# Flamingo-style block (gated cross-attention, MLP, two FFNs) on Trainium2: value split and row moments of the first stage moved to other engines and a later place

## The reference

```python
def layer0_attention(x, y):                # x is normalised per row first: (x - mean) / sqrt(var + 1e-5)
    q = (x @ Wq + bq)                      # 16 heads of 16
    k = (y @ Wk + bk)                      # 77 context rows
    v = (y @ Wv + bv)
    attn = softmax(q @ k.T / 4)            # per head
    out = attn @ v
    return relu(out @ W1 + b1) @ W2 + b2
# then: layer 0 FFN on fp4-quantised operands; layer 1 attention (own Wq, Wk, Wv, Wo, no biases);
# layer 1 FFN: 8 experts, top 2 per row
```

## Time and profile before

| | |
|---|---|
| Runs | 739.12, 739.69, 741.12 us |
| Profiled execution | 739.43 us, span 737.7 us |
| TensorE busy (PE) | 590.7 us, 80% |
| VectorE busy (DVE) | 542.5 us, 74% |
| ScalarE busy (ACT) | 348.6 us, 47% |
| GpSimd busy (POOL) | 250.2 us, 34% |

### The profile page before, as it was taken

The page is one execution under the profiler, slowest core; times in us unless marked ns, Lnnn a source line. Parts: engine busy times, 40 slices in busy tenths (PEclk is TensorE's granted clock), DMA queues, the critical chain, the costliest instruction groups (busy, mean ns, idle before and its releaser), DMA issues. The chain is left out here.

```text
span 737.7 us, 15590 instructions
## 1 busy us (share of the span) xinstructions
PE 590.7 (80%) x5555; PEld 527.1 (71%) x5555; DVE 542.5 (74%) x1117; ACT 348.6 (47%) x865; POOL 250.2 (34%) x253
## 2 busy tenths in 40 slices
PE   4559999899624799999966999998662999999950
PEld 3238999799513688888865899987661889989940
DVE  5958898668995699999882778886568764555537
ACT  2256776523135545554432656555154555555520
POOL 2536767800200000000010556665202475555420
PEclk9999999999955799999996899999655899999985
DMA  8020000030000000000000000000394122222229
GB/s 233 4 65 1 4 2 3 2 118 0 1 0 0 1 1 1 0 1 1 1 1 0 2 2 2 2 4 2 119 381 149 46 80 79 79 74 80 70 73 308
DMA packets 27637, 36.75 MB, mean 50 GB/s; under 512 B 4024, under 2 KB 22265, under 8 KB 27438
## 3 DMA queue, kind: packets, MB, share of 16 engines
q1 hardware_dynamic: 23822, 25.56, 10.7%
q0 software_dynamic: 3744, 10.23, 4.5%
HBM read 26.47 MB, written 9.31 MB: 49 GB/s over the span
## 5 line engine op out<-in xcount | busy, mean ns | idle before, releaser
L940 POOL TENSOR_TENSOR rstd<-mv,eps_col 128x16 f32<-128x16 f32 (+2 forms) x6 | 1.3, 209 | 263.1 <-DVE mv L472 263.1
L970 POOL TENSOR_TENSOR p_lo<-prob,p_hi 128x616 f16<-128x616 f32 x64 | 87.1, 1362 | 5.1
L964 POOL CAST p_hi<-prob 128x616 f16<-128x616 f32 x64 | 44.6, 696 | 68.3 <-ACT prob L1093 68.3
L1021 POOL DMA_INDIRECT y_rows<-rn,dst_row x39 | 43.1, 1106 | 54.8 <-DVE rn L889 53.6
L1093 ACT ACTIVATE prob<-prob 128x616 f32<-128x616 f32 x64 | 45.9, 718 | 32.9 <-DVE prob L575 32.9
L1101 ACT ACTIVATE pT<-ps 128x512 f32<-128x512 f32 (+1 forms) x96 | 46.8, 522 | 25.8 <-PE ps L1426 25.4
L575 DVE TENSOR_TENSOR prob<-ps,smax 128x308 f32<-128x308 f32 x128 | 55.3, 474 | 2.2
L1017 POOL DMA_INDIRECT xin<-x_rows,src_row x39 | 38.2, 979 | 52.6 <-DVE dst_row L856 41.0
L461 DVE CAST ehT_hi<-ehid 128x512 fp32r<-128x512 f32 x39 | 16.6, 427 | 53.0 <-ACT ehid L1317 52.7
L570 DVE TENSOR_REDUCE smax<-ps 128x8 f32<-128x616 f32 x64 | 50.5, 790 | 0.8 <-PE ps L1410 0.8
L1303 ACT ACTIVATE eh<-ps 128x512 f32<-128x512 f32 x39 | 23.3, 597 | 57.6 <-PE ps L1342 57.5
(11 more groups left out here) (282 smaller groups left out, 2013.9 us busy)
## 6 DMA issues: line engine op xcount, KB each, us to landing
el_w<-in_L_ffn_W_dram SPq DMA_DIRECT2D x16, 512.0 KB, 9.8
eh_w<-y_rows SPq DMA_DIRECT2D x16, 256.0 KB, 5.9
x_sb<-in_x_dram SPq DMA_DIRECT2D x4, 512.0 KB, 8.1
x_rows<-rn SPq DMA_DIRECT2D x4, 512.0 KB, 10.1
out_dram<-x_sb SPq DMA_DIRECT2D x16, 128.0 KB, 3.6
stage<-in_L_xattn_W_dram SPq DMA_DIRECT2D x2, 512.0 KB, 3.9
eb<-in_L_ffn_b_dram SPq DMA_DIRECT2D x1, 1024.0 KB, 10.0
w<-in_L_ffn_w_down_dram SPq DMA_DIRECT2D x1, 704.0 KB, 7.8
```

What stands on the lines that cost most here:

```text
L964: pool.tensor_copy(p_hi[:, t % 2, c], prob[:, t % 2, c]).then_inc(s["hi"], 1)
L970: pool.tensor_tensor(p_lo[:, t % 2, c], prob[:, t % 2, c], p_hi[:, t % 2, c], ALU.subtract).then_inc(s["lo"], 1)
L1021: pool.indirect_dma_start(y_rows, bass.IndirectOffsetOnAxis(ap=dst_row[:, j:j + 1], axis=0), ey[:, j % YRING], None) .then_inc(y_out[j % Y ...
```

## The change

Three parts of the first stage are done elsewhere or in another order.
- Loads: context and keys go first, then `k_mask`, `ident`, `head_mask`, then values and the rest; the unused `stage_sel` is no longer loaded; the table has a semaphore of its own.
- Keys: the products of layer 1 go to banks 4 and 5, so that all four follow one another. GpSimd starts its spreading when both halves of layer 1 are split.
- Values: ScalarE casts a value block out of PSUM to bf16; TensorE subtracts the cast from the block in its bank by a product with a negative identity in f16 (`less_h`); ScalarE casts what is left, and so twice more. VectorE has no part in it. The copies of `head_mask` on VectorE (517) go ahead of the keys.
- Blocks: ScalarE masks layer 1 in blocks 0 to 13, VectorE in blocks 14 to 19. The remainders of Wq of layer 1 and Wo go to GpSimd.
- Moments: only row tiles 0 to 3 are done in the first stage. Tiles 4 to 7 follow in VectorE's step -2 of attention of layer 0, tiles 8 to 15 two by two in steps 0, 1, 3 and 4, with aggregates in steps -2, 1 and 4. GpSimd makes rstd and shift for four tiles at a time (`early_rows`): ahead of the MLP weights, before tile 3 and before tile 6. `normalise` waits for its tiles' rows.

```diff
+SOON = 4
+ACT_BLOCKS = 14
...
+        less_h = sb("less_h", [P, P], F16, att)
...
@@ sync @@
-            sp.dma_start(ident[:, :], I["c_ident"]).then_inc(ld["const"], 16)
-            sp.dma_start(head_mask[:, :, :], I["c_head"].rearrange("p (j s) -> p j s", s=NH_MAX)).then_inc(ld["const"], 16)
-            sp.dma_start(k_mask[:, :], I["c_kmask"]).then_inc(ld["const"], 16)
-            sp.dma_start(stage_sel[:, :], I["c_sel"]).then_inc(ld["const"], 16)
             sp.dma_start(ctxT[:, :, :], I["ctxT"].rearrange("(k p) m -> p k m", p=CP)).then_inc(ld["ctx"], 16)
...
             sp.dma_start(bk_col[:, :], I["L0_xattn_bk_cols"]).then_inc(ld["k"], 16)
+            sp.dma_start(k_mask[:, :], I["c_kmask"]).then_inc(ld["const"], 16)
+            sp.dma_start(ident[:, :], I["c_ident"]).then_inc(ld["const"], 16)
+            sp.dma_start(head_mask[:, :, :], I["c_head"].rearrange("p (j s) -> p j s", s=NH_MAX)).then_inc(ld["const"], 16)
...
@@ vector @@
+            dve.wait_ge(kp["zero"], 1)
+            for j in range(PT):
+                dst = vbd[:, :, :, j, 0, :].rearrange("p a b (s c) -> p (a b) s c", c=SLOT)[:, :, :, HD]
+                ch.done(dve.tensor_copy(dst, bcast(head_mask[:, j, :], 1, 2 * B)))
...
-                    src = ps[:, hf, 0:B * M]
+                    src = ps[:, 4 * n + hf, 0:B * M]
...
-            for n in range(2):
-                for b in range(B):
-                    g = 2 * n + b
-                    dve.wait_ge(kp["v_ready"], g + 1)
-                    v = ps[0:M, V_BANK[g], 0:D]
-                    ch.link(dve.tensor_copy(v3[:, g, 0], v))
-                    ch.link(dve.tensor_tensor(v_rest[:, 0], v, v3[:, g, 0], ALU.subtract))
-                    ch.link(dve.tensor_copy(v3[:, g, 1], v_rest[:, 0]))
-                    ch.link(dve.tensor_tensor(v_rest[:, 1], v_rest[:, 0], v3[:, g, 1], ALU.subtract))
-                    dve.tensor_copy(v3[:, g, 2], v_rest[:, 1]).then_inc(kp["v3_ready"], 1)
...
+            dve.wait_ge(ld["x0"], 16)
+            for t in range(SOON):
+                moments(t)
+            aggregate(0, last=SOON)
+            hi, lo, at = splits[0]
+            dve.wait_ge(act_done, 1)
+            ch.done(dve.tensor_tensor(lo, stage[:, at], two_parts(hi), ALU.subtract))
             for g in range(B):
                 for j in range(PT):
                     at = g * PT + j
-                    if at < TILES:
-                        if at % 4 == 0:
-                            dve.wait_ge(ld[f"x{at // 4}"], 16)
-                        moments(at)
-                    elif at == TILES:
-                        aggregate(0)
                     dve.wait_ge(kp["b_ready"], at + 1)
...
-                    dve.tensor_tensor(dst, src, hm, ALU.mult).then_inc(kp["b_used"], 1)
-
-            for n, (hi, lo, at) in enumerate(splits):
-                dve.wait_ge(act_done, n + 1)
-                ch.done(dve.tensor_tensor(lo, stage[:, at], two_parts(hi), ALU.subtract))
+                    ins = dve.tensor_tensor(dst, src, hm, ALU.mult)
+                    if at >= ACT_BLOCKS:
+                        dve.wait_ge(kp["c_ready"], at + 1)
...
+                        ins = dve.tensor_tensor(dst, src, hm, ALU.mult)
+                    ins.then_inc(kp["b_used"], 1)
...
                     step(k)
+                    if n == 0 and k == -2:
+                        dve.wait_ge(ld["x1"], 48)
+                        for t in range(SOON, 2 * SOON):
+                            moments(t)
+                        aggregate(0, first=SOON, last=2 * SOON)
+                    if n == 0 and k in (0, 1, 3, 4):
+                        for t in range(8 + k // 3 * 4 + k % 3 * 2, 10 + k // 3 * 4 + k % 3 * 2):
+                            moments(t)
+                    if n == 0 and k in (1, 4):
+                        g = 2 + k // 4
+                        aggregate(0, first=SOON * g, last=SOON * (g + 1))
@@ gpsimd @@
+            def early_rows(g):
+                inverse_deviation(0, g + 1, first=SOON * g, last=SOON * (g + 1))
+                shift_rows(0, 0, 2 * g + 1, first=SOON * g, last=SOON * (g + 1))
+
+            pool.wait_ge(kp["kT_ready"], 2)
             for hf in range(2):
-                pool.wait_ge(kp["kT_ready"], hf + 1)
...
-            inverse_deviation(0)
-            shift_rows(0, 0, 1)
+            early_rows(0)
+            for n, (hi, lo, at) in enumerate(splits):
+                if n:
+                    pool.wait_ge(act_done, n + 1)
+                    pool.tensor_tensor(lo, stage[:, at], two_parts(hi), ALU.subtract)
             barrier(pool, 1)
...
                 for t in range(TILES):
+                    if n == 0 and t in (3, 6):
+                        early_rows(2 + t // 6)
                     if t:
                         low_half(n, t - 1, 1)
...
+            early_rows(1)
             mlp_weights(0, w1_hi, w1_lo)
@@ scalar @@
-            act.wait_ge(ld["v"], 64)
+            act.wait_ge(ld["const"], 48)
+            act.activation(ident_h[:, :], ident[:, :], ACT.Copy)
+            act.activation(neg_ident[:, :], ident[:, :], ACT.Copy, scale=-1.0)
+            act.activation(less_h[:, :], ident[:, :], ACT.Copy, scale=-1.0)
+            act.wait_ge(kp["table"], 16)
             act.activation(spread[:, :], stage[0:M, 2:5, :].rearrange("p a n -> p (a n)")[:, 0:HM], ACT.Copy)\
                 .then_inc(kp["spread"], 1)
+            for g in range(2 * B):
+                act.wait_ge(kp["v_ready"], g + 1)
+                act.activation(v3[:, g, 0], ps[0:M, V_BANK[g], 0:D], ACT.Copy).then_inc(kp["cast"], 1)
             act.wait_ge(ld["q"], 64)
             for hi, _, at in splits:
                 act.activation(hi, stage[:, at], ACT.Copy).then_inc(act_done, 1)
+            for part in range(1, 3):
+                for g in range(2 * B):
+                    act.wait_ge(kp["rest"], 2 * B * (part - 1) + g + 1)
+                    act.activation(v3[:, g, part], ps[0:M, V_BANK[g], 0:D], ACT.Copy)\
+                        .then_inc(kp["cast"] if part == 1 else kp["v3_ready"], 1)
...
                     at = g * PT + j
+                    if at >= ACT_BLOCKS:
+                        continue
                     act.wait_ge(kp["c_ready"], at + 1)
...
                     att_wait(act, n, "xt", p)
+                    if n == 0:
+                        act.wait_ge(rs[0], 2 * (2 * p // SOON + 1))
@@ tensor @@
-                    if n:
-                        pe.wait_ge(kp["k_used"], hf + 1)
...
+            def value_less(g, part):
+                pe.wait_ge(kp["cast"], 2 * B * part + g + 1)
+                pe.matmul(ps[0:M, V_BANK[g], 0:D], less_h[0:M, 0:M], v3[:, g, part], start=False, stop=True, skip_group_check=True)\
+                    .then_inc(kp["rest"], 1)
+
+            pe.wait_ge(ld["v"], 48)
             pe.wait_ge(dve_done, 6)
...
+            for g in range(2 * B):
+                value_block(g)
+                if g:
+                    value_less(g - 1, 0)
+            value_less(2 * B - 1, 0)
+            for g in range(2 * B):
+                value_less(g, 1)
+            pe.wait_ge(kp["k_used"], 4)
             pe.wait_ge(kp["v3_ready"], 2 * B)
```

More of the change, by code:

```diff
@@ L298, in build @@
         ld = {n: sem(f"ld_{n}") for n in
-              "const x0 x1 x2 x3 ctx k v q w1 w2 bias gu up d wg rank eb".split()}
+              "const x0 x1 ctx k v q w1 w2 bias gu up d wg rank eb".split()}
         stored = sem("stored")
@@ L307, in build @@
         dve_done, pool_done, act_done = sem("dve_done"), sem("pool_done"), sem("act_done")
-        kp = sems("kp", "k_ready k_used kT_ready v_ready b_ready b_used v3_ready c_ready c_used zero spread")
+        kp = sems("kp", "k_ready k_used kT_ready v_ready b_ready b_used v3_ready c_ready c_used zero spread table cast rest")
         tanh_ready = sem("tanh_ready")
@@ L327, in build @@
         rt = sems("r", "const xn xt full logit logits_out gates prob both rank spread picked rows meta")
-        mo = sems("e", "hi weights low xt xhi xlo up h ht bias relu split down y acc")
+        mo = sems("e", "hi weights xt xhi xlo up h ht bias relu split down y acc")
         block = ctx.enter_context(nc.Block())
@@ L388, in _ @@
             sp.dma_start(bv_row[:, :], I["L0_xattn_bv"].rearrange("(a n) -> a n", a=1)).then_inc(ld["v"], 16)
-            sp.dma_start(stage[0:M, 2:5, :].rearrange("p a n -> p (a n)")[:, 0:HM], I["c_spread"]).then_inc(ld["v"], 16)
+            sp.dma_start(stage[0:M, 2:5, :].rearrange("p a n -> p (a n)")[:, 0:HM], I["c_spread"]).then_inc(kp["table"], 16)
             for n in range(2):
@@ L941, in inverse_deviation, with shift_rows @@
                 pool.tensor_tensor(r, r, eps_col[:, TILES + first:TILES + last], ALU.pow).then_inc(rs[n], 1)
-            pool.wait_ge(ld["const"], 64)
+            pool.wait_ge(ld["const"], 48)
+            def shift_rows(k, n, part, first=0, last=TILES):
+                pool.wait_ge(rs[n], part)
```

(23 more changed lines are left out.)

33 lines of the change are left out of this document (6 added, 27 removed).

## The result

| | before | after |
|---|---|---|
| Runs, median | 739.45 us (739.12 to 741.12, 4 runs) | 730.67 us (728.24 to 732.34, 4 runs) |
| Ratio of the runs | | 0.9862, 95% interval 0.9833 to 0.9891 |
| Profiled execution | 739.43 us, span 737.7 | 728.24 us, span 726.2 |
| Attention of layer 0 starts | 46.14 us | 31.45 us |
| First `p_hi` behind that | 13.15 us | 15.86 us |

The profiled execution of the kernel after is the fastest of its four runs, so what it shows to have gained, 11.5 us of span and 11.2 of time, is more than the median's 8.8.

The account below looks back on a forecast made before the run. VectorE was taken to bound the first stage and TensorE attention of layer 0. First stage -8.9 us, attention +5.45, net -3.45 from 739.43 gives 736.0 us; range 732.8 to 739.5.

Parts of the forecast that it names:

- (a): First stage, order of loads: key bias goes from eighth to fourth, so TensorE starts at 5.4 us, bounds 4.9 and 6.0.
- (b): First stage, TensorE: keys done at 10.0 us, then value blocks 9.7, differences 1.2 and a cast 0.4, to 21.3.
- rival C: Head of attention: TensorE's clock falls in the hole before the first `p_hi`, costing 1.9 us: 737.9 us, chance 0.2.
- (c): First stage, ScalarE: casts, weight splits to 22.5 us, eight casts to 25.0; spread products start at 25.2 instead of 31.89.
- (d): First stage, VectorE: keys from 7.35 us, then moments, aggregates and a weight remainder, all by 24, before TensorE needs it.
- (e): First stage, GpSimd: spreads, early rows and two weight remainders finish at 30.8 us, no longer ending the stage.
- (f): First stage, masked blocks: done at 35.9 us, barrier at 37.2 instead of 46.1, 8.9 us earlier, bounds 8.0 and 9.5.
- (g) to (j): Attention of layer 0: moved moments and early rows delay it 2.85 + 1.3 + 1.0 + 0.3 = 5.45 us.
- B: Later insertions in attention are hidden, or the first stage gains 9.5 us: 733.4 us, chance 0.2.
- A: Whole kernel as the forecast sums it: 736.0 us, ends 734 to 737.4, chance 0.45.
- D: First stage: query weights or spread table land late, holding ScalarE; at 3 us nearly all gain goes, 739 us, chance 0.08.
- E: Attention's ramp: the clock stays low, 15 us or more at half clock, giving 742 us or more, chance 0.07.

Follow-up runs that it names:

- e8: Kernel after with the loads of `k_mask`, `ident` and `head_mask` ahead of context and keys again; 734.1 us, ratio to before 0.9916.
- e4: Kernel after with moments of tiles 4 to 7 in first-stage blocks 0 to 3, tiles 8 to 15 between `x_low` and `q_low`; 726.71 us.
- e1: Kernel after with one wait put back: layer 1 key products wait for VectorE's copy of the same half of layer 0; 737.65 us.
- e7: Kernel after with the value split back on VectorE, without ScalarE's casts and TensorE's differences; 739.65 us, ratio to before 1.000.
- e10: Kernel of e8 with 30 products of a constant row ahead of the keys; 733.57 us, ratio to before 0.9886.
- e3: Kernel after with 20 products of a constant row ahead of the keys; 731.68 us, ratio to before 0.9892.
- e2: Kernel before with 40 products of a constant row into an unused bank ahead of the keys; 739.37 us, ratio 1.000.

## Why the prediction was wrong

**(a) Loads.** Right: the keys started at 5.16 us, forecast 5.4. What I had not seen is that a later start can cost 4.6 us and not 1.4, as in e8's profiled execution, where the clock stayed low.

**(b) TensorE in the first stage: this is the step that failed.** "A layer 0 value block takes 3.0 us (17.37 to 20.35), a layer 1 block half of 3.69", and 0.3 for each difference: 10.9 us from the first value product (10.0) to the end of the last first cast ("free at 20.9"). Measured 6.4 us, ending at 15.8. The prices came from rows where TensorE ran at 1.2 GHz, and I took them over to a stage where it has no hole between 5.2 and 15 us. I weighed the clock only where it could be lost, in rival C, and read the granted 1.00 of the first stage as the upper level, although the value products of the earlier trace rows come 0.43 us apart (8 records in 3.69 us). In the kernel after the same products come 0.21 apart once its clock is up. With the clock low (e8) the stretch took 10.4 us, so 4.0 of the 4.5 us are clock, and 0.5 the differences, which came 0.2 apart, and rounding. In all, attention started 5.8 us earlier than forecast: 0.2 at the start of the keys, 0.4 in the keys, 4.5 in the values, 0.5 up to the spread products and 0.2 behind.

| us | forecast | after | e8, clock low |
|---|---|---|---|
| keys start | 5.4 | 5.16 | 6.54 |
| values start | 10.0 | 9.40 | 10.78 |
| values start to last first cast's end | 10.9 | 6.4 | 10.4 |
| from there to the spread products | 4.3 | 3.8 | 3.8 |
| from the spread products to attention | 12.0 | 11.8 | 11.1 |

**(c), (d), (e), (f).** Right in what waits for what, and in size to 0.5 us: the weight splits and eight casts took 3.8 us up to the spread products (forecast 4.3), the 35 masked copies 7.43, and the blocks and mask rows 11.8 (12.0). The last is a little luck: the blocks ended 0.5 us sooner behind the spread products than forecast, and the mask rows and drain took 1.6 us instead of 1.3. VectorE and GpSimd ended ahead of what needed them. In (d) the start of the keys on VectorE, 7.35, does not follow from its rows: (8.95 - 7.36) behind 5.4 is 7.0; measured 6.56, hidden. The weight remainder that I put at 0.68 or 1.9 us took 1.48, hidden: it started at 17.78 us inside a GpSimd instruction that ran from 17.50 to 18.72, and so stood for the rest of one and not for a whole one. The mask's cast took 0.94 us beside GpSimd's last remainder, and 0.22 in e8, where GpSimd was done: a collision I had not counted. It is what makes the table's last row 0.7 us shorter in e8.

**(g) to (j).** In size right to 0.6 us, and each at its place: forecast 2.85 + 1.3 + 1.0 + 0.3 = 5.45, measured 2.70 + 1.14 + 0.84 + 0.2, 4.86 in all. That the moments are the cause is shown by e4, which leaves all the rest of the change in and takes 4.07 us of it back. "Nothing of it is caught up" held: the distance stayed at 4.85 from tile 5 to 15.

**The end of attention.** Between barrier 2 and barrier 6 the kernel after gained 1.9 us more (375.25 against 377.16) in the profiled execution, without any change in the code there. Of the earlier trace rows, the stretch at 0.50 behind barrier 2 is gone:

```profile
140.00:143.00 3.00, 3.00 (x28) 3.00 (x27) 1.38 (x3) 1.68 (x4) 0.00 (x0) 1.00 0.94 277
```

Over the profiled executions of all twelve kernels this part took 374.7 to 378.9 us, with falls of the clock in different places in most of them. So I count it neither for nor against the change. The four runs of the kernel after spread over 4.1 us, at the same mean granted clock (0.879 to 0.882); 22 runs of the kernel before, beside e1 to e4, spread over 5.3. Where the slower runs lose their time stays open, as they have no trace.

**The sum.** -14.7 at attention's start, +4.86 in attention, -1.9 to barrier 6 and +0.2 in the rest: -11.5 in the span of the profiled execution, -8.8 in the medians. The profiled execution is the fastest of four, and which stages of the other three were longer is not shown.

**The rivals.** B came in by its number, "733.4", more nearly than A, but by neither of its reasons: the later insertions were not hidden. C was given the wrong place and sign for this kernel: TensorE's hole in front of the first `p_hi` was 2.41 us and not 3.4, and the clock did not fall at it. It did, 0.4 to 1.1 us behind the hole's end, in e1, e7 and e10, with holes of 2.60 to 2.81 us, where attention took 108.8 or 108.9 us, so C's price is 1.55 us, forecast 1.9. In the kernel after, e3 and e8 the holes were 1.98 to 2.44 us and the clock stayed up. In the three that lost it the clock had also risen earlier, 12.3 to 13.0 us behind the barrier and not 13.4 to 14.3, so the length of the hole is not shown to be the cause. The rule of the Trainium skill (TensorE: Matmul & The Clock Gate, on the two states) that I cited there works in both directions: the clock also rises once TensorE is kept busy. The traces agree in part. In the kernel after TensorE has no hole from 5.16 us on and the clock rises at 10.7; with 30 products ahead of the keys (e10) it rises at 6.9. But in e8 TensorE has no hole from 6.54 to 21 us, and the clock stays low. That half of the rule decided, in the first stage, and what it takes beyond work without a hole is open. D did not come (the table landed by 11.70 us); E did not come.

## What to carry to other kernels

Before a duration of TensorE is carried over to another order of the work, find out at which clock it was measured, from the distance of its matmuls and not from the column of the granted clock alone, and ask whether the new order closes or opens a hole ahead of it. A stage whose work is a chain through TensorE gains twice when its holes go: e1 and e8 show that one wait, or three loads out of place, cost 5.6 and 4.6 us where the clock stays low, of which only 2.4 and 1.4 are the delay itself; and e8's other runs show that whether it stays low can differ from one execution of a kernel to the next, so one profile is not enough to tell. Closing the hole did not bring the clock up by itself in e8; 30 products ahead of the keys (e10) did, in all four executions by their mean clock. Work that is moved out of a stage belongs where an engine stands still, not only where it is not yet late: the same twelve moments cost 4.9 us of attention behind `q_low` and in the steps that follow, and 0.8 or less with eight of them ahead of `q_low` and four in the first stage's blocks.

## What the runs showed that I had not expected

- Forty products of a constant, with no use, bring the clock up within the head of a kernel, and it fell again in the hole of 3.09 us in which TensorE waits for the copy of the keys (e2: up at 8.7 us, down at 12.1).
- The same products shortened a real chain: 12, 8, 10 and 20 of them in the holes at attention's head took 1.5 us off attention (103.2 to 101.7) and cost nothing at its start.
- The granted clock reads 1.00 until an execution's first recorded change, also where matmuls run at 1.2 GHz: in e1 from 14 to 18 us it shows 1.00 beside ten matmuls in 4.0 us of full work, where the kernel after has ten in 2.0 us (12 to 14 us).

```profile
14.00:18.00 4.00, 4.00 (x10) 1.48 (x9) 3.42 (x15) 0.59 (x2) 1.96 (x2) 1.00 0.90 279
```
